# An expert FFN on lists sorted by one expert each, in two passes of 70 tiles, in place of 92 tiles of a pair of experts

## What is computed

```
logits = xt @ Wr + br ; probs = softmax(logits)
top_p, top_idx = top_k(probs, 2) ; weights = top_p / top_p.sum(-1)
xn = (xt - mu) * rsqrt(var + eps)
h  = gelu((xn * ln_g[e] + ln_b[e]) @ W1[e] + b1[e])      # 128 -> 512
y  = h @ W2[e] + b2[e]                                    # 512 -> 128
out = xt + sum over the two experts of weight * y
```

## Time and profile before

| | |
|---|---|
| median of 3 runs | 1132.47 us (1131.96 to 1133.61) |
| the profiled execution, its own time | 1132.14 us |
| its span, first to last instruction | 1129.9 us |
| busy, share of the span: PE, DVE, ACT, POOL | 81%, 61%, 55%, 53% |
| mean granted TensorE clock | 0.854 of full |

### The profile page before, as it was taken

The page is one execution under the profiler, slowest core; times in us unless marked ns, Lnnn a source line. Parts: engine busy times, 40 slices in busy tenths (PEclk is TensorE's granted clock), DMA queues, the critical chain, the costliest instruction groups (busy, mean ns, idle before and its releaser), DMA issues.

```text
span 1129.9 us, 29421 instructions
## 1 busy us (share of the span) xinstructions
PE 916.5 (81%) x8716; PEld 817.8 (72%) x8717; DVE 684.5 (61%) x2173; ACT 616.2 (55%) x1311; POOL 593.5 (53%) x728
## 2 busy tenths in 40 slices
PE   3789997665798466447399999999999999999995
PEld 2677996454798355311289899899899889899895
DVE  5674102997601799673166676676676666766764
ACT  2688212453211454401277777777777767777773
POOL 4463001443271886787456556555655555655653
PEclk9999655789655687655599999999999999999998
DMA  9994003573011245424111111111111111111100
GB/s 256 321 275 118 9 1 106 158 222 111 15 55 43 85 138 165 143 77 163 48 37 47 38 42 46 36 45 37 38 43 42 39 39 36 43 42 35 25 25 1
DMA packets 103811, 91.63 MB, mean 81 GB/s; under 512 B 20166, under 2 KB 85223, under 8 KB 103771
## 3 DMA queue, kind: packets, MB, share of 16 engines
q1 hardware_dynamic: 75332, 65.17, 19.8%
q0 software_dynamic: 9984, 17.35, 4.5%
q10 hardware_dynamic: 18456, 8.67, 2.7%
HBM read 61.38 MB, written 33.40 MB: 84 GB/s over the span
## 4 chain that ended last, share of the span: by engine, by line
PE 55%; DVE 12%; issue 12%; POOL 10%; ACT 8%; DMA 1%; DVEq 1%; SPq 0%; ACTq 0%; POOLq 0%
POOL row_dram L440 6%; PE ps L1175 6%; PE ps L1177 5%; PE ps L1176 5%; PE ps L1196 5%; PE ps L1197 5%; PE ps L1046 5%; PE ps L1090 5%; PE ps L1199 5%; PE ps L1089 4%; ACT AB L661 4%; PE ps L1086 3%; PE ps L1153 3%; ACT AB L660 2%; DVE stats L853 2%
## 5 line engine op out<-in xcount | busy, mean ns | idle before, releaser
L997 DVE TENSOR_TENSOR AB<-AB 128x512 f16<-128x512 f32 x368 | 259.5, 705 | 166.4 <-ACT AB L661 165.2
L494 POOL DMA_INDIRECT out<-B x184 | 193.0, 1049 | 235.5 <-issue 235.5
L660 ACT ACTIVATE AB<-ps 128x512 f32<-128x512 f32 x368 | 221.5, 602 | 91.9 <-issue 64.3
L1196 PE MATMUL ps<-PPb,AB 128*128 x1472 | 243.7, 219 | 0.0
L1197 PE MATMUL ps<-PPb,AB 128*128 x1472 | 243.6, 219 | 0.0
L661 ACT ACTIVATE AB<-ps 128x512 f16<-128x512 f32 x368 | 222.8, 605 | 0.0
L1199 PE MATMUL ps<-PPb,AB 128*128 x1472 | 202.4, 219 | 0.0
L1175 PE MATMUL ps<-B,PPb 128*128 128x256 f16 x736 | 201.8, 274 | 0.2 <-issue 0.2
L1176 PE MATMUL ps<-B,PPb 128*128 128x256 f16 x736 | 201.8, 274 | 0.0
L1177 PE MATMUL ps<-B,PPb 128*128 128x256 f16 x736 | 201.8, 274 | 0.0
L419 POOL TENSOR_TENSOR rs<-vv,half 128x12 f32<-128x12 f32 (+2 forms) x40 | 76.2, 1907 | 133.1 <-DVE vv L877 87.7
(11 more groups left out here) (238 smaller groups left out, 1690.0 us busy)
## 6 DMA issues: line engine op xcount, KB each, us to landing
PPb<-in_L_conv_protein_pair SPq DMA_DIRECT2D x32, 512.0 KB, 6.6
B<-row_dram SPq DMA_DIRECT2D x92, 136.0 KB, 2.1
rows<-in_x SPq DMA_DIRECT2D x32, 256.0 KB, 6.4
g_dram<-work ACTq DMA_DIRECT2D x32, 256.0 KB, 2.4
work<-g_dram SPq DMA_DIRECT2D x32, 256.0 KB, 2.8
ABT<-in_x SPq DMA_DIRECT2D x32, 256.0 KB, 2.9
row_dram<-work SPq DMA_DIRECT2D x29, 136.0 KB, 1.8
out<-B POOLq DMA_INDIRECT x184, 2.3
```

The source lines that it names most:

```text
L494: pool.indirect_dma_start(out_rows, bass.IndirectOffsetOnAxis(ap=token[:, u, b:b + 1], axis=0), acc[:, u, b, :], None, bounds_check=last_t ...
L660: act.activation(Hf[:, e, q, :], full, ACT.Gelu, scale=1.0 / SCALE)
L997: dve.tensor_tensor(rest[:, part], Hf[:, e, q, :], high[:, part], ALU.subtract).then_inc(h_parts[2 * e + q], 1)
L1196: pe.matmul(o(b), hk(0, k, b), w(0, k), start=False, stop=False)
```

## The change

Every token now stands in two lists: one of the seven that go by its lower expert (0 to 6), one of the seven that go by its higher expert (1 to 7). `NG` = 14 groups take the place of 28 in `choose`, which also writes the token's place in the second list into its row (`POS`, a place that was unused).

The FFN runs in two passes of `TP` = 70 tiles. In the first, the row has 136 floats; the lower expert's result is added to it in place in `Rw`, and the whole row, now with the normalized x behind it (264 floats, 1056 bytes), is written by indirect DMA to its place in the second list, in `row2_dram`. In the second, the tile is loaded with the normalized x, the higher expert's result is added, and 128 floats are written to the output. SP starts the second pass's first load only when all stores of the first have landed.

The norm goes from POOL to DVE and is done in the first pass only; POOL's copy of the token numbers is gone (the index is read in the row itself). The row ring is 10 tiles, those of the transposed x and of the hidden values 5. The order is written by `two_lists`: PE does transposes of n, `up` of n-2, `down` of n-4; DVE norm of n, `xT_low` of n-1, `low` of n-3, `mix` of n-5. A loop body holds 10 tiles, and each pass has 10 tiles ahead of its loop. PE's order has two transposes for each tile of one expert. Pad rows are written by 16 DMAs in place of 29, the pad is set by POOL before its last loop, and the counts for it are given by DVE inside the last `choose`. The small input table of pairs is gone.

The core of the diff ("..." marks what is left out):

```
-NPAIR = NE * (NE - 1) // 2
+NL = NE - 1
+NG = 2 * NL
...
-RING = 4
-TILES = -(-((N + NPAIR * (TR - 1)) // TR) // RING) * RING
+RING = 10
+TP = -(-((N + NL * (TR - 1)) // TR) // RING) * RING
+ROWS = NL * CAP + TR
...
-R1, RS, SH, WLO, WHI, TOK = range(D, D + 6)
+R1, RS, SH, WLO, WHI, TOK, POS = range(D, D + 7)
+XN = ROW
+ROW2 = ROW + D
...
+def two_lists(eng, stages, before=None):
+
+    longest = max(lag for lag, _ in stages)
+    assert longest + 2 <= RING and TP % RING == 0
+    for p in range(2):
+        first = p * TP
+
+        def fixed(t0, t1):
+            for t in range(t0, t1):
+                if before and t % RING == 0:
+                    before(first + t)
+                for lag, stage in stages:
+                    if 0 <= t - lag < TP:
+                        n = first + t - lag
+                        stage(n, n % RING, n // RING, p)
+
+        fixed(0, RING)
+        with eng.Fori(first // RING + 1, (first + TP) // RING) as i:
+            if before:
+                before(i * RING)
+            for v in range(RING):
+                for lag, stage in stages:
+                    stage(i * RING + (v - lag), (v - lag) % RING, i + (v - lag) // RING, p)
+        fixed(TP, TP + longest)
...
-        Hp = ABf[:, 4096:8192].bitcast(f16).rearrange("p (s r k t) -> p s r k t", s=4, r=2, k=HC)
+        Hp = rows[:, :, :].rearrange("p j r -> p (j r)")[:, 0:RING // 2 * 2 * H].bitcast(f16).rearrange(
+            "p (s r k t) -> p s r k t", s=RING // 2, r=2, k=HC)
         Bf = B[:, :, :].rearrange("p j c -> p (j c)")
-        Rw = Bf[:, 0:RING * RB * ROW].rearrange("p (s b r) -> p s b r", s=RING, b=RB)
-        xn = Bf[:, 1088:2112].rearrange("p (s b d) -> p s b d", s=RING, b=RB)
-        xTp = Bf[:, 2112:2624].bitcast(f16).rearrange("p (s r t) -> p s r t", s=2, r=2)
-        acc = Bf[:, 2624:3648].rearrange("p (s b d) -> p s b d", s=RING, b=RB)
-        token = Bf[:, 3648:3648 + RING * RB].bitcast(u32).rearrange("p (s b) -> p s b", s=RING)
+        xTp = Bf[:, 0:RING // 2 * TR].bitcast(f16).rearrange("p (s r t) -> p s r t", s=RING // 2, r=2)
+
+        Rw = flat[:, 8192:8192 + RING * RB * ROW2].rearrange("p (s b r) -> p s b r", s=RING, b=RB)
...
+            sp.wait_ge(s.pad_set, 2)
+            lists = ((row_dram, ROW), (row2_dram, ROW2))
+            for rows_of, width in lists:
+                sp.dma_start(rows_of[NL * CAP:ROWS, :].rearrange("(p b) r -> p b r", b=RB), pad[:, :, 0:width]).then_inc(s.pads_out, 16)
+            for v, (rows_of, width) in enumerate(lists):
+                _, counts = nc.values_load_multi_w_load_instructions(nti[0:1, 1, v * NL:(v + 1) * NL], [mybir.EngineType.SP],
...
+                for g in range(NL):
+                    sp.dma_start(rows_of[bass.ds(counts[g] + g * CAP, TR), :].rearrange("(p b) r -> p b r", b=RB),
+                                 pad[:, :, 0:width]).then_inc(s.pads_out, 16)
...
+            def load_tile(n, u, c, p):
+                if isinstance(n, int) and n == TP:
+                    for v in range(RING):
+                        sp.wait_ge(o_stored[v], 16 * RB * (TP // RING))
+                elif not isinstance(n, int) or n >= RING:
+                    sp.wait_ge(o_stored[u], c * (16 * RB))
+                first = sp.value_load(first_row[:, bass.ds(n, 1)], min_val=0, max_val=NL * CT)
+                rows_of, width = lists[p]
+                sp.dma_start(Rw[:, u, :, 0:width], rows_of[bass.ds(first * TR, TR), :].rearrange("(p b) r -> p b r", b=RB)).then_inc(r_loaded[u], 16)
+
+            two_lists(sp, [(0, load_tile)])
...
+                    pool.memset(pad[:, :, :], 0.0).then_inc(s.pad_set, 1)
+                    pool.wait_ge(s.pad_set, 1)
+                    pool.memset(pad[:, :, TOK:POS + 1].bitcast(i32), 1 << 20).then_inc(s.pad_set, 1)
...
-            def norm_tile(n, u):
-
...
-                for b in range(RB):
-                    i = pool.tensor_scalar(xn[:, u, b, :], Rw[:, u, b, 0:D], Rw[:, u, b, RS:RS + 1], Rw[:, u, b, SH:SH + 1], ALU.mult, ALU.add)
-                i.then_inc(s.xn_done, 1)
...
-            def store_tile(n, u):
...
+            def store_tile(n, u, c, p):
+
                 pool.wait_ge(s.y_done, n + 1)
                 pool.sem_inc(s.store_next, 1)
                 for b in range(RB):
+                    if p == 0:
+                        pool.indirect_dma_start(row2_dram, bass.IndirectOffsetOnAxis(ap=Rw[:, u, b, POS:POS + 1].bitcast(u32), axis=0),
+                                                Rw[:, u, b, :], None, bounds_check=last_row, oob_is_err=False).then_inc(o_stored[u], 16)
+                    else:
+                        pool.indirect_dma_start(out_rows, bass.IndirectOffsetOnAxis(ap=Rw[:, u, b, TOK:TOK + 1].bitcast(u32), axis=0),
+                                                Rw[:, u, b, 0:D], None, bounds_check=last_token, oob_is_err=False).then_inc(o_stored[u], 16)
+
+            two_lists(pool, [(0, store_tile)])
...
+            two_lists(act, [(0, xT_high), (2, gelus)])
...
-                dve.tensor_scalar(c.m12[:, PT, :], c.m12[:, PA, :], -0.5, 1.5, ALU.mult, ALU.add)
+                dve.tensor_scalar(c.m12[:, PT, :], c.m12[:, PA, :], -1.0, float(NE), ALU.mult, ALU.add)
+                dve.tensor_scalar(c.m12[:, PID, :], c.m12[:, PB, :], -1.0, float(NE - 1), ALU.mult, ALU.add)
                 tail(dve.tensor_scalar(c.m12[:, LT, :], c.m12[:, LT, :], -2.0, 1.0, ALU.mult, ALU.add))
-                tail(dve.tensor_tensor(c.m12[:, PID, :], c.m12[:, PT, :], c.m12[:, PB, :], ALU.subtract))
-                tail(dve.tensor_scalar(c.m12[:, PID, :], c.m12[:, PID, :], float(NPAIR - 1), None, ALU.add))
-                gj = [P, NPAIR, nj]
-                tail(dve.tensor_tensor(c.ohp, c.m12[:, PID, :].rearrange("p (o j) -> p o j", o=1).broadcast_to(gj),
-                                       over(IG[:, :], gj), ALU.is_equal))
+
+
+                gj, lj = [P, NG, nj], [P, NL, nj]
+                for v, group in ((0, PT), (1, PID)):
+                    i = dve.tensor_tensor(c.ohp[:, v * NL:(v + 1) * NL, :], c.m12[:, group, :].rearrange("p (o j) -> p o j", o=1).broadcast_to(lj),
+                                          over(IG[:, v * NL:(v + 1) * NL], lj), ALU.is_equal)
+                tail(i)
...
+                if b == len(BATCHES) - 1:
+                    dve.tensor_copy(nti[:, 1, :], run[:, :]).then_inc(s.cnt_done, 1)
                 tail(dve.tensor_tensor(c.rank, c.rank, over(c.base, gj), ALU.add))
                 tail(dve.tensor_tensor(c.rank, c.rank, c.ohp, ALU.mult))
-                tail(dve.tensor_reduce(c.m12[:, PT, :], c.rank.rearrange("p g j -> p j g"), AX.X, ALU.add))
+                dve.tensor_reduce(c.m12[:, PT, :], c.rank[:, 0:NL, :].rearrange("p g j -> p j g"), AX.X, ALU.add)
+                tail(dve.tensor_reduce(c.m12[:, PID, :], c.rank[:, NL:, :].rearrange("p g j -> p j g"), AX.X, ALU.add))
...
+                tail(dve.tensor_copy(rows[:, j0:j1, POS:POS + 1].rearrange("p j o -> p (j o)").bitcast(u32), c.m12[:, PID, :]))
...
+            def norm(n, u, c, p):
+                if p == 0:
+                    dve.wait_ge(r_loaded[u], c * 16 + 16)
+                    for b in range(RB):
+                        i = dve.tensor_scalar(Rw[:, u, b, XN:], Rw[:, u, b, 0:D], Rw[:, u, b, RS:RS + 1], Rw[:, u, b, SH:SH + 1],
+                                              ALU.mult, ALU.add)
+                    i.then_inc(s.xn_done, 1)
+
-            def low(n, u, e):
...
+            def low(n, u, c, p):
+
+                high, rest = (Hp[:, u % 5, r, :, :].rearrange("p k t -> p (k t)") for r in range(2))
+                if not isinstance(n, int) or n >= 5:
+                    dve.wait_ge(s.y_psum, n - 4)
...
+            def mix(n, u, c, p):
+
+                dve.wait_ge(s.y_psum, n + 1)
+                if p:
+                    dve.wait_ge(r_loaded[u], c * 16 + 16)
+                share = WHI if p else WLO
                 for b in range(RB):
-                    i = dve.scalar_tensor_tensor(acc[:, u, b, :], ps[4 + e][:, b * D:(b + 1) * D], Rw[:, u, b, WLO + e:WLO + e + 1],
-                                                 Rw[:, u, b, 0:D] if e == 0 else acc[:, u, b, :], ALU.mult, ALU.add)
-                i.then_inc(s.y_done if e else s.y_first, 1)
-
-            def part(f, e):
-                return lambda n, u: f(n, u, e)
-
-            pipeline(dve, TILES, RING, [(0, xT_low), (1, part(low, 0)), (2, part(mix, 0)),
-                                     (1, part(low, 1)), (2, part(mix, 1))], depth=4)
+                    i = dve.scalar_tensor_tensor(Rw[:, u, b, 0:D], ps[4 + u % 2][:, b * D:(b + 1) * D], Rw[:, u, b, share:share + 1],
+                                                 Rw[:, u, b, 0:D], ALU.mult, ALU.add)
+                i.then_inc(s.y_done, 1)
...
+            two_lists(dve, [(0, norm), (1, xT_low), (3, low), (5, mix)])
...
-            def xT(n, u):
-                pe.wait_ge(s.xn_done, n + 1)
+            def xT(n, u, c, p):
+                if p:
```

(39 more changed lines are left out.)

208 lines of the change are left out of this document (71 added, 137 removed).

## The result

| | before | after |
|---|---|---|
| median of the runs, us | 1132.85 (4 runs, 1131.96 to 1133.61) | 1052.12 (4 runs, 1049.95 to 1053.63) |
| profiled execution, its span, us | 1132.14, 1129.9 | 1051.97, 1050.2 |
| PE busy, us | 916.5 (81%) | 815.2 (78%) |

The ratio is 0.9286, 95% interval 0.9268 to 0.9304: 80.7 us less. The forecast was 1019.7 us, 112.8 less; the time lies in the range of 1005 to 1055, near its upper end, and 32 us are missing.

What follows compares the result with a forecast made beforehand. PE bounds the FFN; ahead of it waits pass through DVE's choice and POOL's scatter. FFN 424 + 8 + 2 + 15 + 2 = 451 us against 559, less 2.6 and 2.1: 112.7 less, 1019.7 us; range 1005 to 1055.

Steps and rivals of the forecast that it cites:

- FFN matmuls: PE in the FFN: 140 tiles of one expert at 3.03 us, 424 us, against 92 tiles of two experts.
- Loop tops: PE at loop turns and preloads of both passes: 14 times 0.58 us, 8 us, bounds 0 to 16.
- The other engines: ACT and DVE in a 3.03 us step: 2.80 and 2.9 us; 2 us added for DVE's norm in the first pass.
- Rival 2: First pass: DVE sets the pace at 3.34 us a step, kernel 1040 us; chance 0.1.
- POOL's stores: FFN step: two indirect DMAs take 2.56 us, fit in 3.03 with 0.47 to spare, so add nothing.
- the lock: FFN: POOL's indirect DMA meeting a DVE instruction with two operands from the same memory starts only behind it.
- rival 1: FFN: POOL sets the pace, both DMAs locked 0.35 us, turn 3.26 us, 32 us more, 1052 us; chance 0.2.
- Between the passes: PE stands until first-pass stores land and second-pass loads arrive: 13.6 us plus 1.4 for the low clock, taken as 15.
- The last store: End of the FFN: the last store has the backlog of 2.2 us; 2 us added.
- The choice: Ahead of the FFN, one-hot and scan have half the elements: 2.6 us less in batch 0, 2.1 in batch 1.
- batch 0: First batch of the choice: L810 0.76 us less, scan 1.86 less, PE's `ranks` next in the chain, 2.6 us off.
- Rivals 3 and 4: FFN: 3, DVE's locks make POOL's turn 4.38 us, 1209 us, chance 0.03; 4, PE's steps still wait, 1070, chance 0.07.

Runs made afterwards that it cites:

- e1: The changed kernel with PE's FFN written out without a loop, register loads still at every tenth tile: 1043.63 us.
- e8: The changed kernel with ACT's weights of choice batch 0 made behind its second half's copies of ABT instead of ahead: 1048.45 us.
- e5: The changed kernel with the experts' list in blocks of 16 values, each register load at a multiple of 64 bytes, loop kept: 1022.79 us.
- e6: The changed kernel with the experts' list moved by two values (8 bytes), nothing else: 1049.17 us, one run.
- e7: The changed kernel with the experts' list moved by one value (4 bytes), no load at a multiple of 16 bytes: 1082.97 us, one run.

## Why the prediction was right in part, and where it failed

**FFN matmuls: right.** 3.03 us were forecast, 2.98 measured: 2.76 as priced from the earlier trace rows, and 0.22 for a pair of transposes in place of 0.27. 140 x 0.05 = 7 us better than forecast. PE is 100% busy in the steady rows above.

**Loop tops: the step that failed.** "14 times the 0.58 us of rows 3" was misread to begin with: the row at 816.48 has in brackets 0.46 us of waiting that is put down to POOL's norm. Every second tile of before has such a wait (its intervals there are 5.79, 6.17, 5.79 and 6.37 us), so a top added only 0.2 to it. The 0.6 that e1 shows for a turn is near 0.58 by chance. The step also took the price from a kernel whose loads fell at multiples of 32 bytes and had 12 values. The new list is indexed by single values and loaded from every tenth, 40 bytes on, so every second load begins 8 bytes behind a multiple of 16 and takes 3.5 to 4.0 us; the others have two values over. 40.2 + 3.3 us were measured in place of 8, some 70% of it by the place and count of the loads: with those put right, the excess is 12.4 us with the loop and 2.1 without. My bounds of 0 to 16 didn't hold it, since they came from a turn that costs "nothing or twice that", and not from what is done in a top. A part of it is the clock: behind each of after's six long stands it was 0.50, and the next step took 1.5 to 2.7 us more, 12 us in six cases.

**The other engines.** ACT and DVE fit, as forecast. DVE's norm costs 0.3 us (two in 0.59), and both passes have the same step of 2.98, so the 2 us for a tight DVE were not needed. Rival 2 falls.

**POOL's stores: right in the sum, the lock was real.** POOL's and DVE's timelines of the first pass:

```profile
605.18 0.98 POOL L510 DMA_INDIRECT row_dram<-PPb  x1 [0.30 <-issue]
606.47 1.39 POOL L510 DMA_INDIRECT row_dram<-PPb  x1 [0.30 <-issue]
608.17 0.98 POOL L510 DMA_INDIRECT row_dram<-PPb  x1 [0.30 <-issue]
```

```profile
606.32 0.69 DVE L1023 TENSOR_TENSOR rows<-AB,rows 128x512 f16<-128x512 f32 x1
608.36 0.59 DVE L1007 TENSOR_SCALAR PPb<-PPb 128x128 f32<-128x128 f32 x2
```

The DMA at 606.47 starts in an L1023 (two operands from SBUF, 606.32 to 607.01) and ends at 607.86, 0.85 behind it. Of the 126 DMAs that start between 560 and 775 us 54 start in an L1023, with a mean of 1.35 us (second pass, 815 to 1030: 61 of 131, 1.36). Of the other 72, five start in the last instant of an L1013, just ahead of an L1023, and are long too; the rest take 0.98, also those that start in an L1032 or L1013, which have one operand in PSUM. 0.98 + 0.30 + 1.39 + 0.30 makes 2.97: a locked DMA ends where the next finds a gap, and POOL's turn settles at PE's step. So half of rival 1's lock of 0.35 a DMA came (0.17 in the mean: 1.15 against 0.98), and the slack of 0.47 took it, as argued against it. That the time is the rival's 1052 us is chance. Whether a norm on DVE locks POOL stays open: no DMA began inside one.

**Between the passes: right in size, its parts less so.** 15 us were forecast. From the last matmul at 789.68 to the first `up` at 804.46 are 14.8:

```profile
795.61 0.98 POOL L510 DMA_INDIRECT row_dram<-PPb  x1 [0.30 <-issue]
```

```profile
798.48 3.82 SPq L392 DMA_DIRECT2D PPb<-row_dram  x4
```

```profile
789.68 0.27 PE L1220 MATMUL ps<-PPb,rows 128*128 x2
801.06 0.69 PE L1176 MATMUL ps<-Wr_ident,PPb 128*128 128x128 f32 x2 [11.10 <-DMA PPb<-row_dram]
803.97 0.69 PE L1176 MATMUL ps<-Wr_ident,PPb 128*128 128x128 f32 x2 [0.73 <-DMA PPb<-row_dram]
804.46 0.42 PE L1197 MATMUL ps<-B,PPb 128*128 128x256 f16 x1
```

The last DMA ends 6.9 us behind the start of PE's last matmuls (forecast: 0.6 + 0.8 + 2.2 + 1.3 = 4.9): the backlog was larger, since from 789.18 to the one above six of POOL's DMAs follow every 1.29 us. SP issues the load 1.9 behind that end (2.3 for the landing); the third transposes come 5.5 later and the first `up` 0.5 behind them, 6.0 where 4.2 + 1.2 + 0.3 + 0.7 = 6.4 were taken. 14.8 stand against 13.6 without the clock, and the low clock, taken at 1.4, comes on top of both (802 to 806 at 0.50): 1 us more. **The last store:** its DMA starts at 1040.36, 5.9 us behind the last matmul's, before the change 3.0; 2.9 more against 2 forecast.

**The choice: right in size, wrong in its parts.** The last scatter starts at 544.97 in place of 549.01, 4.0 us sooner; forecast 4.7. (Kernels with the same new choice differ in this time by up to 3 us, so agreement to 1 us is partly luck.) "PE's `ranks` is next in the chain" was wrong for batch 0: PE was still in its transposes, so of the 3.2 us that DVE was early, 2.3 became a wait for PE (e8). POOL's scatter began 1.4 us sooner in place of 4.7: its wait ends at 446.99 + 7.32 = 454.31, before at 446.68 + 9.01 = 455.69. The rest came where I had written "nothing": beside batch 2. Those 64 scatters were locked less. Their long ones before were 1.81 and 1.93 us at 484 to 488 and 5.81 at 498.88; in after only one exceeds 1.7:

```profile
494.26 5.00 POOL L472 DMA_INDIRECT row_dram<-rows,idx  x1 [0.30 <-issue]
```

They are busy for 2.4 us less in sum, and the pad's memsets, some 0.3, are out of the way. Of the 2.4 us 0.8 is chance: this DMA and the one at 498.88 met the same unchanged DVE operation of 4.88 us, 0.7 us behind its start here and 0.1 ahead of it before. The rest is that DVE operations that got shorter held POOL for less time.

Together: of the forecast 112.7 us the loop tops took 35.5 and gap, last store and choice 1.0, 0.9 and 0.7; the better step gave 7 and the norm's unused allowance 2. That leaves 83.6 less, against 80.2 in the profiled executions (1132.14 and 1051.97). Four smaller terms make up the rest. From the last scatter to the first `up` 9.8 us passed (544.97 to 554.80) in place of 8.2 (549.01 to 557.23), 1.6 more, where 0.3 for the third load was left out as within the error. The two passes took 3.0 us more than 70 steps of 2.98, the tops and the counted low clock make (554.80 to 789.68 and 804.46 to 1034.50). From the last DMA's start to the end of the span are 9.9 us, before 8.9: 1.0 more. Against that the FFN of before took 560.9 us (557.23 to its last matmul at 1118.11) and not 559: 1.9 more were to be gained. The 559 came near by luck, since the mean of four tiles is 6.03 and not 6.08 and three long waits for POOL's norm, at 574, 720 and 914 us, are not in it. e5, with its loads in line, takes 1022.8 us, 3 above the forecast, by other parts than the forecast had: its excess is 12.4 us where 8 were taken. Rivals 3 and 4 fall: POOL's turn is 2.97, and PE waits for nothing between the steps.

## What to carry to other kernels

When a list in SBUF feeds registers, lay it out so that every load begins at a multiple of 16 bytes and takes a multiple of four values; check the TENSOR_LOAD rows of the engine that the kernel is bound by. The multiple of 16 bytes is what e6 and e7 show; that of four values rests on the fit. When a step is costed "per turn" from the old kernel, list what a turn does, with the address and size of each access, and see which of them the change alters. Before a difference between two steps is called the price of a turn, take out the wait that the row has in brackets. A stand of some 3 us on PE can cost more than itself, when the clock falls behind it: 1.5 to 2.7 us more in the next step here.
